# Grouped expert product: where lone samples lie, and two passes instead of three for them

## The reference

```python
ids = randint(0, 16, (128,))                      # one expert per sample
y    = einsum('bsi,boi->bso', x, weight[ids])     # x: 128 x 64 x 1024, weight: 16 x 1024 x 1024
h    = einsum('bsd,nrd->nbsr', y, lora_A)         # 8 adapters of rank 16
lora = einsum('nbsr,nor->bso', h, lora_B * (2 * lora_weights)[:, None, None])
out  = x + einsum('bsd,od->bso', y, W) + bias + lora
```

## Time and profile before

| | |
|---|---|
| median of 3 runs (lowest to highest) | 1511.55 us (1508.47 to 1513.35) |
| the profiled execution, its own time | 1511.33 us |
| its span, first to last instruction | 1509.7 us |
| PE busy | 1492.8 us, 99% |
| DVE / ACT / POOL busy | 788.1 / 393.2 / 464.4 us |
| moved by DMA | 257.90 MB, 171 GB/s over the span |
| mean granted clock of PE | 0.999 |

### The profile page before, as it was taken

One profiled execution on the slowest core, in us unless ns is written; L12 is line 12 of the kernel. 1 busy time (PEld: TensorE's weight loads), 2 busy tenths in 40 slices (PEclk: granted clock), 3 DMA queues, 4 the chain that ended last, 5 costly groups with the idle time before them and its releaser, 6 DMA issues.

```text
span 1509.7 us, 29738 instructions
## 1 busy us (share of the span) xinstructions
PE 1492.8 (99%) x6354; PEld 1190.2 (79%) x6355; DVE 788.1 (52%) x1192; ACT 393.2 (26%) x493; POOL 464.4 (31%) x651
## 2 busy tenths in 40 slices
PE   7999999999999999999999999999999999999998
PEld 4878888888888888878788888888888888888887
DVE  7767766367777368378842333333333333333331
ACT  5244343234444244244430111111111111111110
POOL 4365433533344433534102121221211212212111
PEclk9999999999999999999999999999999999999999
DMA  9979866667787467469744555555555555555553
GB/s 279 293 202 246 221 170 164 186 185 201 202 228 197 142 185 189 156 202 239 192 148 130 142 143 140 136 148 140 133 145 141 138 143 139 144 141 134 146 139 84
DMA packets 172705, 257.90 MB, mean 171 GB/s; under 512 B 31616, under 2 KB 135552, under 8 KB 172672
## 3 DMA queue, kind: packets, MB, share of 16 engines
q1 hardware_dynamic: 128896, 138.62, 36.5%
q10 hardware_dynamic: 23360, 73.28, 16.4%
q0 software_dynamic: 20416, 45.65, 10.9%
HBM read 181.93 MB, written 75.50 MB: 171 GB/s over the span
## 4 chain that ended last, share of the span: by engine, by line
PE 94%; DVE 3%; DMA 1%; ACT 1%; issue 1%; SPq 0%; DVEq 0%; POOL 0%; ACTq 0%; POOLq 0%
PE ps L751 31%; PE ps L755 31%; PE ps L758 31%; DVE w_turn L529 1%; DMA a_sb<-in_L_ffn_lora_A_dram 1%; DMA weff<-fold_sb 1%; DVE w_lo L586 1%; DVE fold_sb L644 1%; DVE x_turn L617 0%; ACT x_hi L409 0%; ACT w_hi L401 0%; PE ps L731 0%; DVE x_lo L624 0%; ACT fold_sb L441 0%; SPq L215 0%
## 5 line engine op out<-in xcount | busy, mean ns | idle before, releaser
L751 PE MATMUL ps<-w_hi,x_hi 128*128 (+1 forms) x2096 | 533.4, 395 | 2.9 <-issue 2.9
L755 PE MATMUL ps<-w_hi,x_lo 128*128 (+1 forms) x2096 | 531.4, 394 | 0.0
L758 PE MATMUL ps<-w_lo,x_hi 128*128 (+1 forms) x2096 | 531.2, 394 | 0.0
L751 PEld LDWEIGHTS ps<-w_hi,x_hi 128*128 128x128 f32 x2096 | 392.8, 188 | 101.8 <-issue 5.4
L755 PEld LDWEIGHTS ps<-w_hi,x_lo 128*128 128x128 f32 x2096 | 392.5, 187 | 97.0
L758 PEld LDWEIGHTS ps<-w_lo,x_hi 128*128 128x128 f32 x2096 | 392.2, 187 | 96.8
L208 POOL DMA_DIRECT2D x_raw<-in_x_dram x560 | 299.1, 534 | 399.8 <-DVE x_turn L617 240.9
L617 DVE STREAM_TRANSPOSE x_turn<-x_raw 128x256 f32<-128x256 f32 x544 | 193.7, 415 | 421.8 <-DMA x_raw<-y_scr 363.8
L409 ACT ACTIVATE x_hi<-x_turn 128x512 fp32r<-128x512 f32 x272 | 166.9, 630 | 686.3 <-DVE x_turn L617 670.6
L384 POOL TENSOR_TENSOR stage<-stage,w_place 128x1024 f32<-128x1024 f32 x64 | 153.1, 2392 | 612.0 <-DMA stage<-in_x_dram 612.0
L624 DVE TENSOR_TENSOR x_lo<-x_turn,x_hi 128x512 fp32r<-128x512 f32 x272 | 180.4, 691 | 128.7 <-ACT x_hi L409 124.2
(11 more groups left out here) (71 smaller groups left out, 40.0 us busy)
## 6 DMA issues: line engine op xcount, KB each, us to landing
w_place<-in_L_cond_weight_dram SPq DMA_DIRECT2D x480, 128.0 KB, 4.4
y_scr<-stage ACTq DMA_DIRECT2D x72, 512.0 KB, 4.3
x_raw<-in_x_dram POOLq DMA_DIRECT2D x560, 64.0 KB, 3.8
x_raw<-y_scr SPq DMA_DIRECT2D x512, 64.0 KB, 2.4
stage<-in_x_dram SPq DMA_DIRECT2D x128, 256.0 KB, 3.7
out_dram<-stage ACTq DMA_DIRECT2D x126, 256.0 KB, 3.0
weff<-fold_sb POOLq DMA_DIRECT2D x8, 512.0 KB, 9.9
w_place<-weff SPq DMA_DIRECT2D x32, 128.0 KB, 3.3
```

The source lines that it names most:

```text
L751: mm(ps[b][:, cols], x_hi[b][:, t, :], hi[t], start=t == 0, stop=False)
L755: mm(ps[b][:, cols], x_lo[b][:, t, :], hi[t], start=False, stop=False)
L758: last = mm(ps[b][:, cols], x_hi[b][:, t, :], lo[t], start=False, stop=t == KT - 1)
```

## The change

Places are now packed without gaps up to slot 48 (FLEX): an expert still begins at an even place, but no slot is left empty; the empty slots all come behind slot 48, one after every two used slots, until the spare ones are used up. Slots 4 to 47 (SOLO; on PE a loop over slots 4 to 47) may be lone ones and get another form:

- The second sample that is loaded is the lone sample itself (table `twin`, made from `alone` and `own`).
- VectorE's subtract is split by columns: the upper 64 go to x_lo as before, the lower 64 go to x_lo for a pair but into x_hi's own lower columns for a lone sample. The address is chosen by a table read, without a branch. So the lone tile holds x_hi in rows 0 to 63 and x_lo in rows 64 to 127.
- PE runs two passes, this tile times w_hi and times w_lo. `solo_products` waits for both halves of x_lo before it starts.
- The lower 64 rows of the product are to be added to the upper 64. A lone sample is always the last of its expert. So at each opening of an expert ACT copies the slot before it to its stage buffer and its lower rows to low_rows, which is the second w_turn buffer, and DVE adds (`join_y`) between the first weight chunk and its subtract; for a pair the sum goes to a place that nobody reads. Other slots are copied in two halves.
- The routing has more steps, and its group of four small products takes the place of one.

The steps of the second stage are unchanged. The diff, without declarations:

```diff
+    FLEX = SLOTS - 3 * (EXPERTS // 2)
+    SOLO = range(RING, FLEX)
...
+        x_both = nc.alloc_sbuf_tensor_at("x_both", [P, 2 * RING, KT, P], f32r, offset=ring)
+        x_hi = [x_both[:, 2 * b, :, :] for b in range(RING)]
+        x_lo = [x_both[:, 2 * b + 1, :, :] for b in range(RING)]
...
+        rows_by = sb("rows_by", [P, (2 + TURN) * D], f32)
+        stage = [rows_by[:, b * D:(b + 1) * D] for b in range(2)]
+        w_turn = [rows_by[:, (2 + b) * D:(3 + b) * D].rearrange("p (t m) -> p t m", m=P) for b in range(TURN)]
+        low_rows = rows_by[0:TOK, 3 * D:4 * D]
...
-            sample = entry(eng, slot_sample, 2 * n + h, SAMPLES - 1)
-            if not (isinstance(n, int) and n < RING):
+            late = not (isinstance(n, int) and n < RING)
+            sample = entry(eng, *((twin, n) if late and h else (slot_sample, 2 * n + h)), SAMPLES - 1)
+            if late:
...
+            pool.wait_ge(tables, 3)
...
+            def move_and_round(slot, u, g):
+                opens = entry(act, slot_opens, 2 * (slot + 1), 1)
+                with act.If(opens > 0):
+                    rank = entry(act, slot_rank, 2 * (slot + 1), EXPERTS - 1)
+                    y_room(slot, u, g)
+                    nc.scalar.activation(stage[u % 2][:, :], ps[u][:, :], COPY)
+                    act.wait_ge(w_ready, rank * CHUNKS + CHUNKS)
+                    nc.scalar.activation(low_rows, ps[u][TOK:P, :], COPY).then_inc(copied, 1)
+                    round_w(rank + 1, (rank + 1) % 2)
+                with act.Else():
+                    y_room(slot, u, g)
+                    nc.scalar.activation(stage[u % 2][:, 0:HALF], ps[u][:, 0:HALF], COPY).then_inc(copied, 1)
+                    nc.scalar.activation(stage[u % 2][:, HALF:D], ps[u][:, HALF:D], COPY).then_inc(moved, 1)
+                act.wait_ge(copied, slot - (RING - 1))
+                store_y(slot, u)
...
-            with act.Fori(1, SLOTS // RING) as g:
+            round_x(RING + AHEAD, AHEAD)
+            round_next_expert(RING)
+            with act.Fori(1, FLEX // RING) as g:
+                for u in range(RING):
+                    slot = g * RING + u
+                    round_x(slot + (1 + AHEAD), u)
+                    move_and_round(slot, u, g)
...
-            link(tsc(opens[:, :], ids_f[:, :], 0.5, leads[:, 0:1], ALU.is_gt, ALU.mult))
+            link(tsc(marks[:, 0:1], ids_f[:, :], 0.5, leads[:, 0:1], ALU.is_gt, ALU.mult))
+            link(tsc(marks[:, 2:3], marks[:, 0:1], leads[:, 0:1], 2.0, ALU.subtract, ALU.mult))
+            link(cp(odd_i[:, :], mine[:, 1:2]))
+            link(tsc(odd_i[:, :], odd_i[:, :], 1, None, ALU.bitwise_and))
+            link(tsc(marks[:, 1:2], odd_i[:, :], -2.0, 1.0, ALU.mult, ALU.add))
             opened_step = step[0]
-            link(tsc(half_i[:, :], mine[:, 0:1], ids_f[:, 0:1], 1.0, ALU.add, ALU.add))
-            link(tsc(half_i[:, :], half_i[:, :], 1, None, ALU.arith_shift_right))
-            link(cp(half_f[:, :], half_i[:, :]))
-            link(tsc(vals[:, 5:6], half_f[:, :], 2.0, mine[:, 1:2], ALU.mult, ALU.add))
+            link(tt(order[:, :], mine[:, 0:1], mine[:, 1:2], ALU.add))
+            link(tsc(at_order[:, :], iota_f[:, 0:SAMPLES], order[:, 0:1], None, ALU.is_equal))
...
+            dve.wait_ge(ranked, 1)
+            link(tsc(place[:, :], ps[0][:, HALF + 1:HALF + 2], 2.0, order[:, 0:1], ALU.add, ALU.add))
+            link(tsc(gaps_i[:, :], place[:, :], float(2 * FLEX), None, ALU.max))
+            link(tsc(gaps_i[:, :], gaps_i[:, :], 2, None, ALU.arith_shift_right))
+            link(tsc(most[:, :], ps[0][:, HALF + 2:HALF + 3], -0.5, float(FLEX // 2 + EXPERTS // 2 - 1), ALU.mult, ALU.add))
+            link(cp(gaps_f[:, :], gaps_i[:, :]))
+            link(tsc(gaps_f[:, :], gaps_f[:, :], most[:, 0:1], float(-FLEX // 2), ALU.min, ALU.add))
+            link(tsc(vals[:, 5:6], gaps_f[:, :], 2.0, place[:, 0:1], ALU.mult, ALU.add))
             link(tsc(at_pos[:, :], iota_f[:, 0:POS], vals[:, 5:6], None, ALU.is_equal))
...
+            link(tsc(alone[:, :], ps[2][0:1, HALF:HALF + SLOTS], -1.0, 1.0, ALU.mult, ALU.add))
...
+                    if solo:
+                        if h == 0:
+                            pair = entry(dve, slot_used, 2 * n + 1, 1)
+                        tt(x_lo[b][:, ts, 0:TOK], x_turn[h][:, :, 0:TOK], x_hi[b][:, ts, 0:TOK], ALU.subtract)
+                        lows = x_both[:, bass.ds(pair + 2 * b, 1), ts, TOK:P].rearrange("p a t m -> p (a t) m")
+                        tt(lows, x_turn[h][:, :, TOK:P], x_hi[b][:, ts, TOK:P], ALU.subtract).then_inc(x_ready, 1)
+                    else:
+                        tt(x_lo[b][:, ts, :], x_turn[h][:, :, :], x_hi[b][:, ts, :], ALU.subtract).then_inc(x_ready, 1)
+            def join_y(slot, u):
+                dve.wait_ge(copied, slot - RING)
+                pair = entry(dve, slot_used, 2 * slot - 1, 1)
+                tt(rows_by[0:TOK, bass.ds(pair * ((3 - u % 2) * D) + u % 2 * D, D)], ps[u][0:TOK, :],
+                   low_rows, ALU.add).then_inc(moved, 1)
+            def prepare_next_expert(slot, joined=None):
                 opens = entry(dve, slot_opens, 2 * slot, 1)
                 with dve.If(opens > 0):
                     rank = entry(dve, slot_rank, 2 * slot, EXPERTS - 1)
-                    prepare_w(rank + 1, (rank + 1) % 2)
+                    if joined is None:
+                        prepare_w(rank + 1, (rank + 1) % 2)
+                    else:
+                        turn_w(rank + 1, 0)
+                        join_y(slot, joined)
+                        split_w(rank + 1, (rank + 1) % 2, 0)
+                        dve.wait_ge(moved, slot)
+                        prepare_w(rank + 1, (rank + 1) % 2, range(1, CHUNKS))
                 with dve.Else():
                     dve.nop()
...
+            pairs = slot_sample.rearrange("a (n h) -> a h n", h=2)
+            link(tt(own[:, :], alone[:, :], pairs[:, 0, :], ALU.mult))
+            tt(twin[:, :], own[:, :], pairs[:, 1, :], ALU.add).then_inc(tables, 1)
...
-            for slot in range(1, RING):
+            for slot in range(1, RING + 1):
                 n = slot + AHEAD
                 if slot > 1:
-                    prepare_x(n, n % RING, n % RING, x_index(n))
+                    prepare_x(n, n % RING, n % RING, x_index(n), solo=True)
                 prepare_next_expert(slot)
-            with dve.Fori(1, SLOTS // RING - 1) as g:
+            with dve.Fori(0, (FLEX - 2 * RING) // RING) as g:
                 for u in range(RING):
-                    slot = g * RING + u
-                    v = u + AHEAD
-                    prepare_x(slot + AHEAD, v % RING, v % RING, g + x_index(v))
-                    prepare_next_expert(slot)
-            for u in range(RING):
-                slot = SLOTS - RING + u
+                    n = g * RING + (2 * RING + u)
+                    prepare_x(n, u, u, g + x_index(2 * RING + u), solo=True)
+                    prepare_next_expert(g * RING + (RING + 1 + u), u)
+            for slot in range(FLEX - AHEAD, FLEX + 1):
                 n = slot + AHEAD
-                if n < SLOTS:
-                    prepare_x(n, n % RING, n % RING, x_index(n))
-                else:
-                    prepare_x(n, n % RING, n % RING, (n - SLOTS) // RING, [y_loaded], 2 * QUADS)
+                prepare_x(n, n % RING, n % RING, x_index(n))
+                prepare_next_expert(slot, (slot - 1) % RING)
+            with dve.Fori(0, (SLOTS - FLEX) // RING - 1) as g:
+                for u in range(RING):
+                    n = FLEX + RING + u
+                    prepare_x(g * RING + n, u, u, g + x_index(n))
+                    prepare_next_expert(g * RING + (n - AHEAD))
+            for slot in range(SLOTS - AHEAD, SLOTS):
+                n = slot + AHEAD
+                prepare_x(n, n % RING, n % RING, (n - SLOTS) // RING, [y_loaded], 2 * QUADS)
                 prepare_next_expert(slot)
...
-            mm(ps[0][:, HALF:HALF + 1], more[:, :], opens[:, :], start=True, stop=True).then_inc(ranked, 1)
+            mm(ps[0][:, HALF:HALF + 2], more[:, :], marks[:, 0:2], start=True, stop=False)
+            mm(ps[0][:, HALF + 1:HALF + 2], ones[:, :], marks[:, 2:3], start=False, stop=True)
+            mm(ps[0][:, HALF + 2:HALF + 3], ones[:, :], marks[:, 1:2], start=True, stop=False)
...
+            mm(ps[2][0:1, HALF:HALF + SLOTS], vals[:, 3:4], at_pos[:, :].rearrange("p (n h) -> p h n", h=2)[:, 1, :],
+               start=True, stop=True)
...
+            def solo_products(b, par, n, ready):
+                pe.wait_ge(x_ready, n * 2 + 2)
+                for half in range(2):
+                    cols = slice(half * HALF, (half + 1) * HALF)
+                    hi = [w_hi[:, bass.ds(par, 1), t, cols].rearrange("p a m -> p (a m)") for t in range(KT)]
+                    lo = [w_lo[:, bass.ds(par, 1), t, cols].rearrange("p a m -> p (a m)") for t in range(KT)]
```

(59 more changed lines are left out.)

22 lines of the change are left out of this document (11 added, 11 removed).

## The result

| | before | after |
|---|---|---|
| median (lowest to highest) | 1511.52 us (6 runs beside after) | 1522.88 us (1518.92 to 1525.51, 6 runs) |
| ratio to before | | 1.0078, 95% interval 1.0066 to 1.009 |
| span of the profiled run | 1509.7 us | 1520.6 us |

The change made the kernel 11.4 us slower. The forecast was 1488.5 us, with a range of 1484 to 1498.

A forecast was written before the change was run, and what follows sets the result against it. PE (TensorE) was taken as the bound, busy 99% of the span. The terms -22.4 - 4.5 + 0.5 + 2.9 + 0.5 = -23.0 us gave 1488.5 us for the median, range 1484 to 1498.

The forecast's parts named there:

- part 4: VectorE, tiles 4 to 47: extra 1.1 us a tile, 21.6 us for weights with join; PE stalls 2.9 plus 0.5 us.
- On average it just fits, so the lead decides.: Slots 5 to 47: VectorE needs 456.9 us against PE's 459.2, so its lead over PE decides whether PE waits.
- the prediction's reserve of 14: VectorE's lead after an expert opens: the tile four slots on is ready at 31 us against 44.8 for PE.
- C: Rival: VectorE bounds slots 5 to 47, extra 2.5 us and 6.5 us a tile, about 1543 us; chance 0.04.
- B: Rival: a tile's extra on VectorE is 1.5 us rather than 1.1, reserve used up, 1492.5 to 1500 us; chance 0.20.
- A: Rival: preparation hidden everywhere, no stall at slot 9 or later, no start cost, -26.9 us, 1484.6 us; chance 0.19.
- the start: Longer routing on VectorE and PE makes slot_tab 1.7 us late before slot 0; cost 0 to 1.7, taken as 0.5 us.
- D: Rival: the other branch costs PE as much as the saved pass, so no change, about 1511 us; chance 0.02.
- Part 1: PE, six lone slots: two passes instead of three remove 96 matmuls of 0.2333 us, saving 22.4 us.
- Parts 2 and 3: Hole, wait and low clock at slot 5 vanish, gaining 4.5 us; longer routing before slot 0 costs 0.5 us.
- the 1.1: Extra VectorE time in us per tile 4 to 47: 0.38 for the split subtract, 0.75 for table read and register operations.
- The stall at slot 9: PE wants slot 9 at 131.5 us but x_lo is ready at 134.4: 2.9 us, bounds 0 and 6.

The follow-up runs named there:

- 514: Changed kernel with 9 never executed instructions and their branch ahead of VectorE's loop, now at places 514 to 838 instead of 497 to 821: 1522.38 us, ratio 1.0072.
- 633: Changed kernel with 136 never executed instructions ahead of VectorE's loop, which then stands at places 633 to 957 of its code: 1522.52 us, one run.
- the earlier load: Changed kernel with VectorE's loop moved to places 569 to 893, and the loads of the seventh and eighth tile released two turned weight chunks earlier: 1487.84 us, ratio 0.9847.
- the loop at 569: Changed kernel with a never executed block of 64 instructions ahead of VectorE's loop, now at places 569 to 893 instead of 497 to 821: 1492.16 us, ratio 0.9875.

## Why the prediction was wrong

**The step that failed is in part 4: "On average it just fits, so the lead decides."** VectorE's time for slots 5 to 47 was summed from its instructions, 43 x 5.1 + 11 x 21.6. The cost of going back in the loop was not in it, although the change made that body longer. It is 7 to 9.5 us for each of nine returns. With the measured sizes (below) VectorE needs 43 x 4.4 + 11 x 21.3 + 74 = 498 us against PE's 459.2. Less the prediction's reserve of 14, an estimate of 24 to 25 is exposed, before the clock is counted. Measured were 32 us of waits and slow clock. With the loop moved by an idle branch they shrink to 1 (6.0 - 5.1), while the same branch with another length leaves them (514, 633); with the length and place given to the kernel before, the gaps come. That the length and the place of the loop's code are the cause is shown; that blocks of 128 count and that three blocks of 128 are what is kept is inferred from the table above. It fits every row of the table if the blocks start 75 to 117 instructions off my count: a body of 325 touches only three where it begins within the first 60 of a block, one of 265 within the first 120. Where exactly, and why a return costs as much as it does, stays open.

The Trainium skill (Runtime: NRT & Kernel Launch, "Instruction fetch mechanics") says that a taken branch whose target lies outside a window of two pages forces a fetch before execution goes on, and gives 256 instructions to a block. The mechanism agrees with the gaps and packets here. The window as it states it does not: with two blocks of 256 kept, the costly starts would lie within 68 neighbouring places modulo 256, and 514 (2) and 633 (121) don't. The prediction should have weighed this rule as a rival, since the diff lengthens a loop's body, and did not. No row of before could have priced it.

**Rivals.** None named it. C had the right side, that VectorE holds up PE, but by luck, with a wrong mechanism and size: a tile costs 4.4 us, not 6.5, and VectorE without the gaps keeps up (1492.2 us). B has no ground, for the same reason. A, all hidden at 1484.6, is what the earlier load comes near to: 1487.8, of which the start takes 1.5. D is refuted: each balance closes within 0.1 us with the full 22.4 us for 96 matmuls fewer.

**Part 1** was right, see the counts and balances. **Parts 2 and 3**: -4.5 + 0.5 forecast together; the new places alone gave a span 2.9 us shorter. The hole and its low clock went (3.7 us). The start isn't settled: slot 0 began at 25.60 to 27.41 in the kernels with the new routing and at 25.50 to 26.98 in those with the old one, so the 0.5 lies within what this moment varies by. Five kernels have a wait of 1.0 to 1.5 us ahead of slot 5, which the prediction said would not be there (1.32 at 88.55 in the loop at 569). Tile 5, which it took from before as turned at 83.19, is turned at 85.2 there.

**Part 4, sizes.** The pieces are 423 and 420 ns (forecast 440; the estimate of 424 beside it was nearer). But neighbours start 0.34 us apart, so four take 1.43 us (131.52 to 132.95) where two large ones took 1.34: the split costs 0.1 us, not 0.38. Weights with the join take 159.06 to 180.40, 21.3 us (21.6). Tiles in a backlog, in the loop at 569, start at 129.33 and, four later, at 146.89: 4.4 us, not 5.1. The rest of the 1.1 is the table read, which I charged in full to each tile. Of the extra 0.4 a tile, 0.1 is the split, so at most 0.3 of the forecast 0.75 shows. The last tile of the four:

```profile
146.89 1.43 DVE L676 STREAM_TRANSPOSE x_turn<-x_raw 128x256 f32<-128x256 f32 x4 [0.21 <-DVE x_both L689]
```

**The stall at slot 9**: 2.9 us forecast, 1.85 to 4.87 measured in six kernels. The place was right, the size by luck, and the reason wrong. In the loop at 569 tile 9 was ready at 132.95, not 134.4, and PE came there at 133.46, not 131.5, so x_lo was in time; it was ScalarE's copy of slot 5 behind tile 9's rounding, and PE's table read behind that.

Where the returns cost nothing, the kernel took 1491.6 and 1492.2 us: 3 to 4 us over the forecast of 1488.5, inside its range. The terms named above did not come out one by one, so that nearness is partly luck.

## What to carry to other kernels

When a change lengthens a loop's body, count its instructions on every engine, not only those on the path. The sign here was a gap "issue" once for every pass, ahead of its first instruction, with more instruction packets on the queue that brings the code. Writing the loop out, or moving it to a place that suits its length, took it away; two other places (514, 633) did not, so the move has to be measured. Here that turned 1.0078 into 0.9875 of the time before, and a load released two chunks earlier into 0.9847. A wait that has the forecast size in the forecast place may still have another cause: read the waiting engine's own table reads and the semaphore ahead of them before changing what it seemed to wait for.

## What the runs showed of the hardware

- At a return of a VectorE loop of 325 instructions the engine stood still for 0.6 to 2.1 us at two places. At five others it was 4.6 to 9.5 us (6.5 to 9.5 in the changed kernel), with about five packets of 8 KB. The same loop written out had 19 packets from 150 to 530 us and no gap "issue" over 2.21.
- VectorE's subtracts of 256 columns lasted 420 to 423 ns each, but neighbours started 0.34 us apart.
- A table read on PE's queue took 300 ns or, the next one, 1762 ns (rows above).
- The clock after a wait is not given by the wait's length. Behind 1.85 us (the loop at 514) the granted clock was 0.55, behind 2.16 us (after) and 2.24 us (the loop written out) 0.54 and 0.59, the lower level, 1.2 GHz; behind 2.87 us (the loop at 569) it was 1.00. Windows of the last three, columns as in the earlier trace rows:

```profile
135.75:139.50 3.75, 3.75 (x10) 2.97 (x11) 2.75 (x8) 1.59 (x3) 2.26 (x5) 0.54 1.08 310
```

```profile
137.35:140.50 3.15, 3.15 (x9) 2.49 (x10) 2.81 (x8) 1.66 (x3) 1.78 (x4) 0.59 1.07 293
```

```profile
136.40:140.00 3.60, 3.52 (x15) 2.91 (x16) 2.77 (x8) 2.36 (x4) 2.24 (x5) 1.00 1.04 291
```
